# A graph network on one core: pacing 408 scatters by a matmul loop, moving 24 gathers behind a barrier, and a one-hot built from two tensors

## The reference, cut to what matters

```python
def _softmax_aggregate(msg, dst, n):
    m = jax.ops.segment_max(msg, dst, num_segments=n)
    ex = jnp.exp(msg - m[dst])
    denom = jax.ops.segment_sum(ex, dst, num_segments=n)
    alpha = ex / denom[dst]
    return jax.ops.segment_sum(msg * alpha, dst, num_segments=n)

# block L0, three times: message = relu(x[src]) + 1e-7
out = _softmax_aggregate(msg, dst, n) + x
h = out @ W1 + b1            # 128 -> 256, then batch norm, relu, @ W2 + b2

# block L1, three layers over nodes and edges
h = relu(x @ nw.T);  e = relu(ea @ ew.T)
agg = segment_sum(e, dst)                       # sums of the edge attributes
n2 = relu(concat([agg, h]) @ fnw.T + fnb)
e2 = relu(concat([h[src] + h[dst], e]) @ few.T + feb)

# around them
x = x + L0(relu(layernorm(x)), src, dst)
x = x + L1(relu(layernorm(x)), [src, dst], edge_attr_64)
```

## Time and profile before

| | |
|---|---|
| median of 3 timed runs | 4765.41 us (4755.52 to 4767.22) |
| the profiled execution's own time | 4728.06 us |
| its span | 4726.3 us |
| mean granted TensorE clock | 0.876 |
| PE busy | 3580.1 us (76%) |
| PEld busy | 2372.6 us (50%) |
| DVE busy | 1855.2 us (39%) |
| ACT busy | 1182.7 us (25%) |
| POOL busy | 2633.4 us (56%) |

### The profile page before, as it was taken

The page is one execution under the profiler, slowest core; times in us unless marked ns, Lnnn a source line. Parts: engine busy times, 40 slices in busy tenths (PEclk is TensorE's granted clock), DMA queues, the critical chain, the costliest instruction groups (busy, mean ns, idle before and its releaser), DMA issues.

```text
span 4726.3 us, 73381 instructions
## 1 busy us (share of the span) xinstructions
PE 3580.1 (76%) x22631; PEld 2372.6 (50%) x22631; DVE 1855.2 (39%) x4048; ACT 1182.7 (25%) x2569; POOL 2633.4 (56%) x2750
## 2 busy tenths in 40 slices
PE   2111179996988978888887888988488888888888
PEld 1000046653555555455555555557366666666666
DVE  6000056541221337121227122218255555555555
ACT  1000033220000015000006000007244444544444
POOL 4777700004656656666664666665666666666663
PEclk6555589997999998899998999999799999999998
DMA  6000056555666646666655666665555555555553
GB/s 234 22 7 7 16 175 233 181 181 165 199 203 213 206 150 233 195 201 195 221 180 203 197 196 209 211 187 140 143 135 133 133 133 129 136 131 135 132 133 91
DMA packets 367696, 747.52 MB, mean 158 GB/s; under 512 B 102785, under 2 KB 197659, under 8 KB 366722
## 3 DMA queue, kind: packets, MB, share of 16 engines
q0 software_dynamic: 134912, 331.04, 24.7%
q1 hardware_dynamic: 224679, 362.01, 24.1%
q10 hardware_dynamic: 7899, 51.90, 2.8%
HBM read 613.65 MB, written 131.02 MB: 158 GB/s over the span
## 4 chain that ended last, share of the span: by engine, by line
PE 43%; another core or an unknown queue 19%; issue 18%; DVE 7%; SPq 6%; ACT 2%; DMA 1%; DVEq 1%; POOL 1%; ACTq 1%; POOLq 0%
PE ps L1486 17%; PE ps L1518 7%; PE ps L655 3%; PE ps L643 2%; PE ps L661 2%; SPq L2099 2%; PE ps L647 2%; PE ps L2151 1%; PE ps L2163 1%; SPq L2097 1%; PE ps L2132 1%; PE ps L1837 1%; PE ps L2169 1%; SPq L2096 1%
## 5 line engine op out<-in xcount | busy, mean ns | idle before, releaser
L601 POOL DMA_INDIRECT ring<-split_table,src_idx x1240 | 1181.6, 953 | 1188.5 <-PE ps L661 452.1
L1486 PE MATMUL ps<-spare,acc 128*128 128x500 fp8e4 x5292 | 1196.5, 381 | 185.1 <-issue 78.0
L2122 POOL DMA_INDIRECT ring<-h_table,idx_ring x832 | 837.9, 1007 | 494.0 <-remote 230.2
L1486 PEld LDWEIGHTS ps<-spare,acc 128*128 128x128 bf16 x5292 | 519.5, 99 | 801.8 <-issue 201.3
L1518 PE MATMUL ps<-ring,onehot 128*84 128x256 bf16 x3720 | 486.4, 286 | 90.4 <-issue 89.6
L1587 DVE TENSOR_TENSOR onehot<-onehot,ps 128x168 f32<-128x168 f32 x165 | 54.2, 328 | 1269.6 <-PE ps L1497 770.9
L612 POOL DMA_INDIRECT adjacency<-acc x408 | 416.7, 1021 | 180.6 <-issue 128.6
L1431 ACT ACTIVATE work<-ps 84x256 f32<-84x256 f32 x155 | 58.9, 380 | 1734.6 <-remote 1133.1
L1518 PEld LDWEIGHTS ps<-ring,onehot 128*84 128x84 bf16 x3720 | 426.1, 124 | 124.0 <-issue 118.2
L2132 PE MATMUL ps<-ident,ring 128*128 128x128 f32 x1664 | 271.6, 285 | 86.5 <-DMA acc<-e_few 55.8
L2169 PEld LDWEIGHTS ps<-mats,work 128*128 128x128 f32 x1664 | 235.4, 203 | 128.6 <-issue 128.0
(11 more groups left out here) (329 smaller groups left out, 4710.2 us busy)
## 6 DMA issues: line engine op xcount, KB each, us to landing
acc<-split_table SPq DMA_DIRECT2D x104, 768.0 KB
spare<-adjacency SPq DMA_DIRECT2D x108, 512.0 KB
e_few<-spare SPq DMA_DIRECT2D x104, 512.0 KB
acc<-e_few SPq DMA_DIRECT2D x208, 256.0 KB
work<-in_edge_attr SPq DMA_DIRECT2D x104, 256.0 KB
spare<-rel_rows SPq DMA_DIRECT2D x208, 126.0 KB
split_table<-acc ACTq DMA_DIRECT2D x32, 768.0 KB, 3.3
ring<-split_table,src_idx POOLq DMA_INDIRECT x1240
```

The lines of the kernel that those rows point to most:

```text
L601: e.indirect_dma_start(out=to, out_offset=None, in_=table, in_offset=bass.IndirectOffsetOnAxis(ap=src_idx[:, 2 * i + h, j:j + 1], axis=0)) ...
L1486: ins = e.matmul(ps[2 + 2 * c + kind][:, 0:width], split[j % 2][:, k, q, kind * D:(kind + 1) * D], moving, start=(b == q == 0), stop=(b == ...
L2122: e.indirect_dma_start(out=rows[:, s, j, :], out_offset=None, in_=h_table, in_offset=bass.IndirectOffsetOnAxis(ap=idx_ring[:, s, j:j + 1], ...
```

## The change

Three edits. In `scatters` the first scatter of each group of four waits, beside its old wait, until PE has finished `few_e0` of `pairs_behind(n)` pairs of the attributes' loop: none for groups 0 to 15, 1 pair for group 16, then 9 pairs for each 8 groups, 96 pairs for the last group, 101. The gathers of layer 0's first three pairs leave setup and become the first of layer 0's POOL part; setup's POOL program now waits for the scatters and the stored split table only. And `onehotT` is compared by a `tensor_tensor` of `relb` with `iota_p` broadcast along the row, where it was a `tensor_scalar` with `iota_p` as the scalar of the partition.

```diff
@@ scatters @@
                 if i % EACH == 0 and n >= SCATTERS:
                     e.wait_ge(S(f"gather_spread{n % SCATTERS}"), 16 * EACH * (n // SCATTERS))
+                if i % EACH == 0:
+                    reached(e, S("few_e0"), 2 * pairs_behind(n))
                 e.indirect_dma_start(out=adjacency, out_offset=bass.IndirectOffsetOnAxis(ap=spread_i[:, i:i + 1], axis=0),
...
+        def pairs_behind(n):
+
+            return min(NPAIR, max(0, 9 * n // 8 - 17))
@@ setup, POOL @@
                 scatters(e, S)
-                e.wait_ge(S("src"), 16)
-                e.wait_ge(S("rel_out"), 32)
+                scattered(e, S)
                 split_stored0(e, S)
-                e.wait_ge(S("sums"), NPAIR)
-                e.wait_ge(S("few_e0"), 2 * NPAIR)
-                for i in range(SLOTS3):
-                    pair_gathers(e, S, i, 0)
-                scattered(e, S)
@@ edges, POOL @@
-                for i in range(SLOTS3 if layer == 0 else 0, PAIRS):
+                for i in range(PAIRS):
                     reached(e, S("sums"), free_after(i, whole))
@@ edge layers, DVE @@
-                    e.tensor_scalar(onehotT[:, i.off % 4, :], relb[:, i.off % 4, :], iota_p[0:3 * W, :], None,
+                    e.tensor_tensor(onehotT[:, i.off % 4, :], relb[:, i.off % 4, :], iota_p[0:3 * W, :].broadcast_to([3 * W, GE]),
                                     ALU.is_equal).then_inc(S("one_hotT"), 1)
```

## The result

The changed kernel takes 4418.99 us (median of 4 runs, 4409.16 to 4427.52); the kernel before takes 4764.57 us beside it (4 runs, 4755.52 to 4767.22). The ratio is 0.9278, 95% interval 0.9258 to 0.9297: 345.6 us or 7.2% faster. The forecast was 4425 us.

The account below looks back on a forecast made before the run. Setup was taken to be bound by POOL's indirect DMAs, served at 1.40 us each, whose backlog slows every engine. Terms -329 - 30 + 18 = -341 give 4387 us, plus 37.4 to the runs' median 4425; 8-in-10 range 4335 to 4610.

Parts of the forecast that it names:

- wait: Setup: scatters waiting for PE's pairs end the attributes' loop at 725 us instead of 1053.7, -329 us.
- gathers: Between loop and layer 0: 24 gathers leave setup, PE starts 15 us behind the loop instead of 47.6; -30 us.
- compare: Edge layers: 208 one-hot instructions grow by 0.344 us, +72 us of DVE time, a quarter charged; +18 us.
- The crawl and its cause: Setup: one server takes 1.40 us per indirect DMA of POOL; a backlog of about two slows the other engines.
- The start: Start of setup's loop: first 64 scatters unaffected, POOL pauses until pair 0 is done at 174 us, first matmul at 165.
- The pace of the loop: Attributes' loop: each group of four scatters takes 5.91 us, 85 groups 502 us.
- see-saw: Scatters and loop: a crawl finishes no pair, POOL stands, the backlog drains; loss from layer 0, 1.056 times the server.
- The end: Loop after group 101: eight remaining pairs take 34 us, plus 15 us for the other engines and the clock.
- The 37 us between profile and runs: Whole kernel: the runs' median is 37.4 us above the profiled execution's 4728.06, added to 4387 us.
- A worse see-saw: Rival, scatters and loop: a crawl holds until the backlog is gone, 8.0 us a group, 4587 us; chance 0.16.
- No effect: Rival, setup: the hardware loop or straight-line code causes the crawl, loop end unchanged, -12 us, 4753 us; chance 0.05.
- a scatter that always stops the others: Rival, setup: any scatter in service stops the other engines without a backlog, loop +43 us, 4796 us; chance 0.07.

Follow-up runs that it names:

- e3: The kernel before with only the one-hot compare changed to two tensors; 4764.48 us, ratio 0.9997.
- e4: The kernel before with the scatters' wait and the moved gathers, old compare kept; 4436.86 us, ratio 0.9309.
- e1: The kernel before with only the scatters' wait added; 4459.21 us, ratio 0.9349 to the kernel before.
- e11: The changed kernel without the wait, POOL filling 520 columns of an unread tile behind each scatter; 4397.35 us, one execution, 0.930 of the kernel before.
- 84 columns: The changed kernel without the wait and with the old compare, POOL filling 84 columns behind each scatter; 4681.51 us, 0.990 of the kernel before.

## Why the prediction was right

Total and sign were right; two terms were off and offset each other. By the experiments with one edit each: wait -309 (predicted -329), gathers -37 (-30), compare -4, which is nothing (+18).

**The crawl and its cause.** Right: a wait that keeps PE's work and POOL's indirect DMAs in step removes it, and without the scatters the four slow slices are gone. "One server, 1.40 us for each indirect DMA of POOL, and a crawl once the backlog is about two" is right in that the crawl depends on how close the scatters follow each other, and not on how many there are. As a threshold at 1.40 us it is too sharp: 1.46 us apart still crawls. And the backlog isn't one of DMA transfers, which are through some 2 us after each issue; what the server is stays open, so the cause of the crawl is shown down to "indirect DMAs of POOL too close together" and no further.

**The start.** Predicted: no gap in scatters 1 to 64, a pause from 138 to 174 us, the loop at 165. Measured: 138.91 to 166.37, the loop at 156.6 (its first matmul, put at 165), pair 0 done at 165.5, 8 us early. The clock was up after the first pair, where the 15 us of reserve had been meant for it.

**The pace of the loop is the step that was mis-sized.** "So 5.60 x 1.056 = 5.91 us per group" took the loss of the see-saw from layer 0. Measured is 6.53 us, 1.17 times the server; over 85 groups that is +53 us. What the loop pays beside the crawl, and what the term had no part for, is the lower clock behind a stutter (L667 2.08 us at 314.69 where 1.13 is normal), 0.59 us a pair or 0.66 a group, where the miss is 0.62; whether layer 0 pays it too, and whether four engines taking turns add to it, isn't tested. On POOL's side a group is 5.04 us of issue, and the rest is mostly the 34 stalls (79.1 / 85 = 0.93 us a group, which the prediction hadn't named) and the wait itself, which holds 13 groups and not each one. The end was mis-sized the other way: from group 101 to the loop's end 29.8 us, where 34 + 15 stood. Together -8 + 53 - 19 = +26: 751 us instead of 725. That the gathers' -30 and the compare's +18 missed by 7 and by some 20 us to the other side is luck; without it the forecast would have stood some 20 us too low.

**The gathers.** PE's pause fell to 19.7 us (predicted 15), and 24 gathers in a row made the stutter that was named, from 783 to 790 us. So the first sums start 44.8 us behind the loop's end, where they started 64.7 behind it: -20 in the traces at that point. Timed by itself the edit gives -37, the upper bound, with 13 us of it in the layers by one trace of each kernel.

**The compare.** "I charge a quarter, +18 us" is wrong. 208 x 0.337 = 70 us more of DVE's time disappear whole: e3 0.9997, and the change is not slower than e4, which lacks it. That the compare stands ahead of L2276 in DVE's order was no reason for a charge, since the row that I had for idle time (DVE 173 of 300 us) holds enough of it in front. The Trainium skill ("GPSIMD Engine Reference", Specifications) names contention with GpSimd for VectorE's two-port modes and for two SBUF inputs, as the new form has them; the median of an L2122 gather is 960 ns before and after, the mean 1007 and 1029, and no run here turns that into time of the kernel.

**The 37 us between profile and runs** were added as they stood. The batches suggest what they are: another chip or its condition, mainly in the edge layers. That was harmless as the difference between the kernels is nearly the same on both (0.9278 of 4728 is -341, of 4765 -344).

**The rivals.** A worse see-saw (8.0 us a group): 6.53 lies less than a third of the way from 5.91 there, and 4587 us is far off. No effect, and a scatter that always stops the others, are both excluded, by e1 and by e11: with a scatter every 1.68 us, the packets of each through at the earliest 1.7 us after its issue, the loop ran at its full 4.31 us a pair. The rule of the Trainium skill ("DMA: Bandwidth & Descriptors", Queues, rings and completion order), by which each DMA engine goes round its queues packet by packet, names no distance between instructions, and no run here shows it at work in the crawl: the DMA engines were 2% busy in it before and 9% with 84 columns.

## What to carry to other kernels

If engines of a trace run one instruction per 1.4 us with no wait named and idle DMA engines, look at what GpSimd issues without a pause: indirect DMAs at 1.3 to 1.4 us from each other all but stopped everything here, and at 1.7 us did no harm. Before pacing by a wait for another engine, try plain distance: 0.38 us of idle work behind each scatter gained 8.0%, the wait 7.2%, both with the same other two edits. And an edit that doubles an instruction of an engine with 40% idle time is first to be tested as free.

## What the runs showed of the hardware that I had not expected

- The crawl follows the distance of the indirect DMAs steeply: between 1.40 us on average (1.31 where POOL isn't held up) and 1.68 us the loop went from 148 matmuls in 200 us to 1393, its rate without any.
- The crawl isn't a backlog of transfers: in the kernel before it went on for 25 us in which the DMA queues handled no packet, and from 150 us on each scatter's packets had ended within 3.7 us of its issue.
- A scatter of 64 rows cost what one of 128 rows costs (1.40 us in the crawl), and both made 32 packets, the 16 with the rows half as large.
- A fill of 84 columns (0.18 us) behind an indirect DMA lengthened the distance by 0.05 us only, from 1.26 to 1.31, since 0.13 of POOL's 0.30 us before the next one went away.
- A compare of two tensors, 126 partitions by 512 columns in bf16, took 0.685 us, with a per-partition scalar 0.348, and the kernel's time was the same.
